# Last batch's expert pairs beside its attention, first dense layer begun early, own order tables for first and last batch

## The reference

```python
for attn, ffn in ((L0_attn, L0_ffn), (L1_attn, L1_ffn), (L2_attn, L2_ffn), (L3_attn, L3_ffn)):
    xn = layernorm(x)
    x = x + attn(xn) * silu(ffn(xn))
# layer 1: windows of 32 tokens, 16 heads; per (token, offset, head) two gelu networks -> logits, softmax, weighted values;
#          ffn: top 2 of 8 low-rank experts for a whole row of tokens
# layer 2: causal softmax attention over 64 channels and over 4:1 compressed tokens; ffn: 8 experts, h = relu(x @ W1 + b1), y = h @ W2, top 2
# layer 3: linear attention; ffn: 16 experts of width 64 (top 4) and a shared one, silu(x @ w1) * (x @ w3) @ w2
# layer 4: softmax attention, 16 heads of 8:
out = einsum('bhts,bhsk->bhtk', softmax(q k^T / sqrt(8)), v)
denom = maximum(norm(out, axis=-1).mean(axis=(batch, token)), 1e-5)      # one number per head, over ALL batches
proj = (einsum('bhtk,hkd->bhtd', out / denom, Wo) + bo) * clip(gate, 0, 1); s = proj.sum(heads) / 16
#          ffn: 64 experts of width 64, top 8 within the best 4 of 8 groups, and a shared one
```

## Time and profile before

| | |
|---|---|
| median of 3 runs (lowest, highest) | 3681.01 us (3677.37, 3684.49) |
| the profiled execution: its time / its span | 3681.61 / 3679.8 us |
| mean granted clock of TensorE | 0.891 |
| busy: PE, DVE, ACT, POOL | 83%, 66%, 45%, 16% |
| DMA | 353.80 MB, mean 96 GB/s |

### The profile page before, as it was taken

How to read it: one execution, slowest core, us unless ns; L and a number is a source line. 1 busy time by engine, 2 the same in 40 slices (tenths; PEclk the granted TensorE clock), 3 DMA queues, 4 the chain that set the end, 5 groups by cost and what they waited for, 6 DMA issues and landing times.

```text
span 3679.8 us, 43467 instructions
## 1 busy us (share of the span) xinstructions
PE 3047.4 (83%) x15958; PEld 1508.5 (41%) x16050; DVE 2423.3 (66%) x4577; ACT 1666.6 (45%) x2499; POOL 579.3 (16%) x425
## 2 busy tenths in 40 slices
PE   5569769996899869998699978998699986997579
PEld 1125324553255423554245532454235542455225
DVE  7446966577666875669765786668756697642625
ACT  5325515464354625465154643546254651542143
POOL 2001101401023000311013010230103210130013
PEclk7679979997799969998699987999799997998799
DMA  3320254304441244402553035422445024531244
GB/s 117 139 48 1 66 158 134 96 21 106 125 145 58 46 135 113 143 19 63 144 137 110 21 93 132 142 66 46 135 100 153 21 62 139 142 108 45 55 141 123
DMA packets 226709, 353.80 MB, mean 96 GB/s; under 512 B 32897, under 2 KB 141249, under 8 KB 224897
## 3 DMA queue, kind: packets, MB, share of 16 engines
q1 hardware_dynamic: 226497, 351.02, 34.5%
HBM read 301.70 MB, written 48.61 MB: 95 GB/s over the span
## 4 chain that ended last, share of the span: by engine, by line
PE 48%; issue 22%; DVE 20%; POOL 4%; ACT 3%; DMA 2%; SPq 1%; DVEq 0%; ACTq 0%; POOLq 0%
PE PS L1680 6%; PE PS L1688 6%; PE PS L1849 5%; PE PS L1826 5%; DVE U L906 5%; PE PS L1853 4%; PE PS L1113 3%; PE PS L1794 2%; POOL D L1421 2%; DVE U L899 2%; PE PS L1805 2%; DVE D L1669 2%; PE PS L1250 1%; POOL RS L579 1%; PE PS L1262 1%
## 5 line engine op out<-in xcount | busy, mean ns | idle before, releaser
L1421 POOL TENSOR_TENSOR D<-D,GW 128x512 f32<-128x512 f32 x320 | 429.1, 1341 | 1343.8 <-ACT D L1494 1118.6
L787 ACT ACTIVATE U<-U 128x2048 f32<-128x2048 f32 x256 | 483.9, 1907 | 122.3 <-DVE U L906 66.5
L1664 DVE SCALAR_TENSOR_TENSOR D<-D,PS 128x512 f32<-128x512 f32 x336 | 229.0, 681 | 368.8 <-ACT D L1498 319.9
L1494 ACT ACTIVATE D<-PS 128x512 f32<-128x512 f32 x336 | 200.4, 596 | 538.8 <-PE PS L1849 538.8
L1826 PEld LDWEIGHTS PS<-WST,D 128*128 128x128 f32 (+1 forms) x2688 | 347.0, 194 | 190.2 <-DVE D L1669 107.2
L906 DVE SCALAR_TENSOR_TENSOR U<-PP,RD,QB 128x512 f32<-128x512 f32 x512 | 370.9, 790 | 51.9 <-ACT QB L784 50.2
L1826 PE MATMUL PS<-WST,D 128*128 128x128 f32 (+1 forms) x2688 | 370.3, 281 | 35.5 <-DVE D L1669 35.5
L1853 PE MATMUL PS<-XT,WST 128*128 128x512 f32 (+1 forms) x672 | 358.0, 615 | 20.7 <-DVE D L1664 20.0
L1849 PE MATMUL PS<-XT,WST 128*128 128x512 f32 (+1 forms) x672 | 364.3, 625 | 8.2 <-DMA WST<-in_pairs_dram 6.2
L1615 DVE TENSOR_REDUCE MX<-PS 128x2 f32<-128x1024 f32 x256 | 300.0, 1222 | 97.6 <-PE PS L1772 97.6
L1113 PE MATMUL PS<-U,resident 128*32 128x512 f32 x2048 | 295.6, 683 | 75.7 <-ACT U L787 75.7
(11 more groups left out here) (356 smaller groups left out, 3759.2 us busy)
## 6 DMA issues: line engine op xcount, KB each, us to landing
GW<-gates_scratch SPq DMA_DIRECT2D x320, 256.0 KB, 4.5
WST<-in_pairs_dram SPq DMA_DIRECT2D x336, 192.0 KB, 2.4
U<-band_scratch SPq DMA_DIRECT2D x32, 1280.0 KB, 8.7
UU<-in_w_dram SPq DMA_DIRECT2D x64, 512.0 KB, 5.7
UU<-pad_scratch SPq DMA_DIRECT2D x8, 1792.0 KB
UU<-q_scratch SPq DMA_DIRECT2D x24, 384.0 KB
UU<-k_scratch SPq DMA_DIRECT2D x24, 384.0 KB
e_scratch<-D SPq DMA_DIRECT2D x8, 1024.0 KB, 4.5
```

The costliest lines, as they stand in the source:

```text
L787: e.activation(ring(i), ring(i), ACT.Gelu).then_inc(S["act"], 1)
L1421: e.tensor_tensor(AV[:, n % 3, :], AV[:, n % 3, :], GW[:, p // 2 % GWS, p % 2, :], ALU.mult).then_inc(S["gated"], 1)
```

## The change

- **Tables.** `TURN` goes from 428.30 to 417.95 and all tables are new. The first batch's two threads have tables of their own (`a_first_*`, `b_first_*`), and so has thread b of the last batch (`b_last_*`).
- **Last batch.** A third thread, c, holds the 33 pairs of layer 4 for the last batch alone, with the transposition of their gates ahead. It uses PS banks 0 to 3, free by then, and keeps its two intermediates in VP (`sl`) and QE and QB (`av`). Thread b keeps the attention, and then takes the denominators, the norms, the means and the closing projections, on PZ.
- **Saved batches.** Six of the seven saved batches (three loads each) and the last constants are loaded right behind the first pair weights, while batch 7's dense layer runs; the seventh goes into UU after layer 4's last W3. Before, all stood between the gate loads and the weights of the pairs of layer 4.
- **Waits.** The row of layer 2's gates is copied to XN in place of HT, so that its copy no longer waits for the end of layer 2's attention (`mix`); that wait stands ahead of the update on DVE. The first up waits for the normalised input of layer 2 (`a_xt` 2) in its place.

The number of instructions of each kind is unchanged on each engine. In the order, 28 of the 32 ups of batch 0's dense layer stand ahead of batch 1's first matmul (none did), among the scores of batch 0's layer 2. Of the last batch's 33 pairs, 9 stand between the first and the last S13, two between the last S13 and the first S23, 12 among S23 and W3 and 10 behind.

```diff
-TURN = 428.30
+TURN = 417.95
...
+        VPF = VP[:, :, :, :].rearrange("p j n d -> p (j n d)")
+        late = lambda b, l: b == B - 1 and l == 3
+        pair_ps = lambda b, l, k: PS(k) if late(b, l) else PZ(k)
+        sl = lambda b, l, n: VPF[:, T * (n % 3):T * (n % 3) + T] if late(b, l) else SL[:, n % 3, :]
+        av = lambda b, l, n: (QE[:, 0, :], QE[:, 1, :], QB[:, 0, :])[n % 3] if late(b, l) else AV[:, n % 3, :]
...
-        def thread(part, e, turn):
+        def thread(part, e, turn, batches, name):
...
+        def second_half(part, e, name):
+            yield from thread(part, e, 1, range(1), "b_first_" + name)
+            yield from thread(part, e, 1, range(1, B - 1), "b_" + name)
+            yield from thread(part, e, 1, range(B - 1, B), "b_last_" + name)
+        def last_pairs(part, e, name):
+            yield from thread(part, e, 1, range(B - 1, B), "c_" + name)
...
             for q in range(WS):
                 yield
                 pair_load(e, b, q)
+            if b == B - 1:
+                for k in range(B - 2):
+                    yield
+                    sp_kept(e, k)
...
+            if b == B - 1:
+                yield
+                e.wait_ge(S["pv3"], at("pv3", b, 16))
+                sp_kept(e, B - 2)
...
                 if x == 0:
                     e.wait_ge(S["pv3"], at("pv3", b, 16))
-                    if b == B - 1:
-                        sp_before_final(e)
...
-                    e.wait_ge(S["mix"], at("mix", b, 4))
-                    e.activation(HT(b)[0:E1, :], PZ(3)[0:E1, :], ACT.Copy).then_inc(S["g1_row"], 1)
+                    e.activation(flat(XN(b))[0:E1, :], PZ(3)[0:E1, :], ACT.Copy).then_inc(S["g1_row"], 1)
...
+            e.wait_ge(S["mix"], at("mix", b, 4))
             (yield from dve_update(e, b, 0.5)).then_inc(S["b_x"], 1)
...
                         if x == 0:
+                            e.wait_ge(S["a_xt"], at("a_xt", b, 2))
...
+        def c_pe(e, b):
+            yield
+            e.wait_ge(S["mix"], at("mix", b, 4))
+            e.wait_ge(S["gate_dve"], at("gate_dve", b, 4))
+            for j in range(NT):
+                last = e.transpose(PS(2)[0:E3, P * j:P * j + P], GT[:, j, :], ident)
+            last.then_inc(S["gate_ps"], 1)
+            yield from b_pe_pairs(e, b, 3)
...
-            weave(thread(a_pe, e, 0), thread(b_pe, e, 1))
-            pe_final(e)
+            weave(first_half(a_pe, e, "pe"), second_half(b_pe, e, "pe"), last_pairs(c_pe, e, "pe"))
```

More of the change, by code:

```diff
@@ L1375, in b_sp @@
                 gate_load(e, b, 3, q)
-            for x in range(E1):
+            for x in range(E1 if b + 1 < B else 0):
                 yield
@@ L1825, in down @@
                 for j in range(NT):
[L1826 removed]
+                    last = e.matmul(pair_ps(b, l, 3)[:, P * j:P * j + P], av(b, l, n)[0:m, P * j:P * j + P], WST[0:m, (PAIRS * b + n) % WS, 2, :],
                                     start=(p == 0 and j == 0), stop=(p == npair(l) and j == NT - 1), skip_group_check=True)
@@ L1978, in build, with pe_rotate @@
+        def pe_rotate(e, k):
+            e.wait_ge(S["fin_ys"], k + 1)
+            if k >= 2:
+                e.wait_ge(S["fin_z"], 2 * (k - 2) + 1)
+            for j in range(NT):
+                last = e.transpose(PZ(2 + k % 2)[:, P * j:P * j + P], YS(k)[:, P * j:P * j + P], ident)
+            last.then_inc(S["fin_t"], 1)
         block = ctx.enter_context(nc.Block())
```

320 lines of the change are left out of this document (218 added, 102 removed), and 319 rows, old and new, of the table STARTS.

## The result

| | before | the change | the change's order once more (last experiment) |
|---|---|---|---|
| median, us | 3679.19 (3677.12 to 3684.49, 4 runs) | 3613.01 (3610.45 to 3617.21, 4 runs) | 3620.69 (3616.03 to 3624.70, 4 runs) |
| ratio to before, 95% interval | | 0.9819 [0.9802, 0.9836] | 0.9844 [0.983, 0.9857] |
| span of the profiled execution | 3679.8 | 3610.2 | 3621.7 |

The change is 1.8% faster: 66 us less, where 75 were forecast. The third column is the same sequence of instructions on every engine, measured later on another occasion: 1.6%, 57 us.

What follows compares the result with a forecast made beforehand. No single engine was taken to set the time, so the stages decide. From 3681.6 us, 4 came off for the first batch, 42 for six turns at 7 each and 30 for the last batch: 3606 us, range 3577 to 3650.

Steps and rivals of the forecast that it cites:

- Maxima stage +12.7: Last batch, maxima of layer 4's scores: DVE-bound before and after, 56 us in place of 43.2 with nine pairs added.
- S23 and W3 +26: Last batch, the exponents' stage: with 12 pairs PE needs 70.5 us and bounds it, in place of 44.5.
- the -20: Turn 1, batch 1 beside batch 0: 48 us less PE work ahead of its merge, 140 us in place of 160.8.
- the floor of 124: Turn 1 ahead of its merge: DVE's busy time, 124 of 160.8 us, as the least that stretch could take.
- I take -2: Dense layer's end in each turn: update, normalisation and transposes come up to 2.7 us earlier; 2 us gained.
- "-3" for DVE's gaps: DVE-bound stretch of each turn: gelu items fill PE's wait for layer 3's router; 3 of at most 5.9 us gained.
- "-2" in the third stage: Each turn's chain of transfers and small operations: shorter changes of hands after reordering gates and BAND matmuls, 2 us gained.
- A: Rival: only the ends change and the turns keep their 430.8 us, 3648 us in all; chance 0.15.
- B: Rival: the turns gain 10 us each as the third stage's chain shortens as well, 3583 us; chance 0.17.
- C: Rival: maxima mixed with pairs in the last batch run at clock 0.68, +20 us, 3626 us; chance 0.10.
- D: Rival: slower, as gate loads come late in SyncE's queue and a turn loses 11 us, 3714 us; chance 0.04.
- E: Rival: the pairs don't overlap the attention, since both go through DVE and ACT in order, 3636 us; chance 0.08.

Runs made afterwards that it cites:

- the first part's old order in the change: The change, with turns 2 to 7 in the old order between the 13th gelu item and layer 2's normalisation: 3624.98 us, 0.9860 of the kernel before.
- the second part alone: The kernel before, with the change's order in turns 2 to 7 only from about the first S23 on: 3671.88 us, 0.9982.
- the last and the first part: Two runs: the change with turns 0 to 7 in the old order, 3642.58 us; the kernel before with the change's order in turns 0 and 1, 3677.67 us.
- the turns alone: The kernel before, with the change's copies and waits for layer 2's gate row and its order in turns 2 to 7 only: 3654.65 us, 0.9933.

## Why the prediction was right, and where it was not

**The outcome.** 3606 us was forecast and 3613 measured (3621 in the second set), inside 3577 to 3650; faster, as 0.93 of the chance had it. That it came so close is in part luck. In the table of parts turn 1 gained 9 us and the five turns behind it 6.5 us less than forecast, while the seventh turn and the last batch gained 5 each more; these errors nearly cancel.

**The last batch: stages right, one cause missed.** Maxima stage +12.7, measured +14.1 (57.4 for 43.3). S23 and W3 +26, measured +22.3 (66.1 for 43.8). The rest, 104.2 + 23.6 us in place of 30.5 + 3 + 23.6: -70.7, measured -70.6 (128.5 to 57.9). What failed there is the sentence that the early loads are worth nothing or 6 us. The 104.2 had PE's wait for WST in it, so the sum gave the pairs' overlap what was the loads'. Measured apart, the overlap with the attention is 25.5 us, less than the 30 forecast for it, and 10.9 us stay without it; loads put back ahead of the last weights cost 12.7.

**The first batch: the beginning right, turn 1 short by a stretch that wasn't costed.** +16 forecast, +16.4 measured. In turn 1 the -20 came from the stretch ahead of its merge: that stretch lost 28 us (the merge starts 133 us into the turn, 161 before), the floor of 124 not quite reached. But 8 to 10 us were lost again, most of it behind the first S23, where the turn has an order of its own that I hadn't costed; with the old relation there turn 1 takes 404.7. Turns 0 and 1 together gave 1 us in the profile and nothing measurable in the run of that part alone (2 us, inside its interval), in place of 4 and, with the general -7, 11.

**The six turns: mis-sized.** Of the -7 a turn, 4.3 came, and all three terms were too large at their places.
- "I take -2" for the update: the transposes behind it (L1518, 1680.13 before) start 98.0 us into the turn and did 98.3 before, so 0.3 (0.2 in the mean of 45 turns). With the first part's old order in the change they start at 98.9, so against that the order is worth 0.8 or 0.9. The four inputs left their place between the last sum and the update, but they now stand ahead of that sum, and DVE has to do them first all the same:

```profile
1647.28 4.72 DVE L1119 SCALAR_TENSOR_TENSOR U<-PP,RD,QB 128x512 f32<-128x512 f32 x7
1651.91 2.38 DVE L1759 SCALAR_TENSOR_TENSOR GB<-PS,GT,GB 128x128 f32<-128x128 f32 x8
1654.99 0.69 DVE L818 SCALAR_TENSOR_TENSOR GB<-XN,GB 128x512 f32<-128x512 f32 x1 [0.69 <-ACT XN L1673]
```

- "-3" for DVE's gaps: the stage takes 79.0 for 79.1, with DVE busy 71.8 for 73.2; the gaps grew. In the mean table 1.4 us show ahead of the first S23.
- "-2" in the third stage: 93.1 for 93.9 in these two profiles.

Behind the first S23, where I had costed nothing, 2.9 of the 4.3 us show. There PE is busy 92 to 96% of the stages, and its idle time fell (10.5 us of a turn's last two stages before, 8.1 now). But I can't call the order there the cause: with the first part old 2.4 of the 4.3 go, and the second part alone brings 0.8. What failed is the step of adding up terms place by place. A change of order ahead of the first S23 is worth what is left of it at the end of the turn, and how the two parts share the 4.3 stays open.

**The seventh turn.** "I give it nothing": 5 us shorter. The 6 MB do collide a little, with one wait of 4.77 us for D in layer 3 of the last batch, but the turn gains like the others.

**The rivals.** A (only the ends, 3648) is what the last and the first part give together, some 3641: excluded by the turns alone, -25. B is out: the turns gain 4.3 in the mean. C is out: clock 0.89 in place of 0.7, and the stage's length doesn't hang on it (below). D is out for layer 4 in the turns: there GpSimd's first product waits for ACT (40.5 us, D of L1742). But "I am wrong if GpSimd's first product waits for GW" was too broad a sign. In layer 3 it waits for GW in every batch, 27 to 29 us before and 29 to 31 in turns 2 to 7, and in the last batch's layer 4 it does so in the change (52.04 us, above) and did not before. This cost little: DVE is idle 4.1 us in that whole stage. E (no overlap) is out by the 25.5. The lower bound of 0.9 on the clock among the maxima was missed by 0.01, without consequence.

## What to carry to other kernels

Moving work beside a stage pays what the stage's bounding engine doesn't need for it: nine pairs, 26 us of PE work, were worth 12 us among DVE's maxima, but three pairs more, moved into PE's longest wait, saved nothing: DVE had 3.3 us more to do in the bounded stage, it stood idle there 4.9 us more, 4.2 of them waiting for a pair whose gates landed late, and the chain behind had less cover. So check that what moved work needs is there by then, and what it takes of the engine that bounds the stage. Moving an operation only ahead of another on the same busy engine gained 0.2 to 0.9 us of 2.7 here; look at what the engine has to finish by then. Put bulk loads for the end early: 18 more of them ahead of the last weights in one queue cost 12.7 us. And a gain is not always made where it shows: put back one part at a time, and look at the length of the whole turn.
